# Graph attention and hyperbolic mean on one core: mask work and split parts moved to GpSimd, shorter scalar chains, and another opening of the mean

## The reference, cut to what matters

```python
h = jnp.maximum(_layernorm(x, axis=-1), 0.0)
x = x + _L0_gnn_ref(h, adj, adj, ptr, Wq, bq, Wk, bk, Wv, bv)
h = jnp.maximum(_layernorm(x, axis=-1), 0.0)
x = x + _L1_gnn_ref(h, adj, W)

# layer 0
a = jnp.where(mask, query @ key.T * scale, 0.0)
scores = (a + b + edge_encoding) * jnp.where(mask, 1.0, -1000000.0)
softmax = jax.nn.softmax(scores, axis=-1) * mask
return softmax @ value

# layer 1
XW = mobius_matvec(W, X)                    # scalars: sqrt, artanh, tanh of each point's norms
gamma = jnp.maximum(2.0 / (1.0 + KAPPA * jnp.sum(X * X, axis=-1, keepdims=True)), 1e-15)
denom = _clamp_abs(A @ (gamma - 1.0))
nom = A @ (gamma * X)
two_mean = nom / denom                      # then more scalars of each point
```

## Time and profile before

| | us |
|---|---|
| median of 3 runs | 844.17 |
| lowest and highest run | 841.47, 846.86 |
| profiled execution | 846.85 |
| its span, first to last instruction | 845.0 |

### The profile page before, as it was taken

One profiled execution on the slowest core, in us unless ns is written; L12 is line 12 of the kernel. 1 busy time (PEld: TensorE's weight loads), 2 busy tenths in 40 slices (PEclk: granted clock), 3 DMA queues, 4 the chain that ended last, 5 costly groups with the idle time before them and its releaser, 6 DMA issues.

```text
span 845.0 us, 14675 instructions
## 1 busy us (share of the span) xinstructions
PE 754.9 (89%) x4989; PEld 693.3 (82%) x4996; DVE 667.2 (79%) x1371; ACT 478.9 (57%) x866; POOL 66.0 (8%) x128
## 2 busy tenths in 40 slices
PE   4999889999999997988639699999999999999980
PEld 4888667788778886876538699999999999999980
DVE  6778567887887886878629978888988888888874
ACT  3444366677677676858334355555555555445853
POOL 0000010100010100130200200000000000000080
PEclk9999989999999998998959899999999999999995
DMA  5115276777667774754950859999999999998632
GB/s 137 51 53 223 109 293 220 265 289 285 234 238 252 266 281 161 254 195 102 226 125 1 177 115 208 197 198 202 193 196 193 191 193 190 194 211 177 146 127 75
DMA packets 53574, 157.24 MB, mean 186 GB/s; under 512 B 9232, under 2 KB 30992, under 8 KB 47376
## 3 DMA queue, kind: packets, MB, share of 16 engines
q1 hardware_dynamic: 53520, 156.60, 69.5%
HBM read 148.16 MB, written 8.42 MB: 185 GB/s over the span
## 4 chain that ended last, share of the span: by engine, by line
PE 59%; DVE 20%; DMA 6%; issue 6%; ACT 4%; DVEq 4%; SPq 1%; ACTq 0%
PE bank L630 49%; PE bank L762 5%; DVE least L1458 4%; DMA adjL<-in_adj 3%; DMA adjU<-in_adj 2%; DVE adjT_lo L1398 2%; DVE least L1442 2%; PE bank L696 2%; PE bank L748 1%; DVE X_lo L1378 1%; DVE bank L1390 1%; DVE v L1262 1%; DVE scores L1415 1%; ACT adjT_hi L951 1%; PE bank L622 1%
## 5 line engine op out<-in xcount | busy, mean ns | idle before, releaser
L630 PE MATMUL bank<-X_hi,adjT_hi 128*128 128x258 f32 x1024 | 292.0, 285 | 28.5 <-DVE adjT_lo L1398 28.3
L630 PE MATMUL bank<-X_lo,adjT_hi 128*128 128x258 f32 x1024 | 291.9, 285 | 0.0
L630 PE MATMUL bank<-X_hi,adjT_lo 128*128 128x258 f32 x1024 | 291.3, 284 | 0.0
L630 PEld LDWEIGHTS bank<-X_hi,adjT_hi 128*128 128x128 f32 x1024 | 195.5, 191 | 30.7 <-issue 23.6
L630 PEld LDWEIGHTS bank<-X_lo,adjT_hi 128*128 128x128 f32 x1024 | 196.0, 191 | 0.0
L630 PEld LDWEIGHTS bank<-X_hi,adjT_lo 128*128 128x128 f32 x1024 | 195.8, 191 | 0.0
L762 PE MATMUL bank<-values,probT 128*128 128x256 f32 x512 | 123.1, 385 | 4.4 <-ACT probT L991 4.4
L951 ACT CAST adjT_hi<-turned 128x1024 fp32r<-128x1024 f32 x64 | 67.1, 1048 | 75.9 <-PE bank L630 57.4
L762 PEld LDWEIGHTS bank<-values,probT 128*128 128x128 f32 x512 | 94.5, 193 | 18.2 <-ACT probT L991 5.5
L951 ACT CAST adjT_hi<-bank 128x1024 fp32r<-128x1024 f32 x64 | 64.8, 1013 | 69.3 <-PE bank L630 45.3
L1398 DVE TENSOR_TENSOR adjT_lo<-turned,adjT_hi 128x1024 fp32r<-128x1024 f32 x64 | 77.7, 1215 | 21.7 <-ACT adjT_hi L951 21.5
(11 more groups left out here) (172 smaller groups left out, 1117.6 us busy)
## 6 DMA issues: line engine op xcount, KB each, us to landing
adjL<-in_adj SPq DMA_DIRECT2D x120, 512.0 KB, 8.8
adjU<-in_adj SPq DMA_DIRECT2D x32, 1024.0 KB, 6.1
adjL<-in_adj SPq DMA_DIRECT2D x16, 2048.0 KB, 10.2
x_scratch<-x SPq DMA_DIRECT2D x16, 258.0 KB, 3.6
xin<-in_x SPq DMA_DIRECT2D x8, 512.0 KB, 3.8
xt<-in_x SPq DMA_DIRECT2D x16, 256.0 KB, 4.4
adj<-in_adj SPq DMA_DIRECT2D x8, 512.0 KB, 12.4
x_all<-x_scratch SPq DMA_DIRECT2D x16, 256.0 KB, 11.0
```

What stands on the lines that cost most here:

```text
L630: last = pe.matmul(dst, a[i][a_cols], b[j][b_cols], start=(k_first and n == 0), stop=(k_last and n == 2))
```

## The change

- GpSimd makes `same`, `factor`, `far_part` and the overwritten columns of each lower tile (`mask_lower`), one step ahead; VectorE waits for `s_same` and `s_pushed`.
- The points have two batches of 16 columns. The chain of a batch is written with fewer operations. That of the first batch is spread over steps 11 to 14: two parts between the second and third read of scores, four between `tiles_out` and `maximum_lower`. Its 16 pieces are scaled and split wholly by GpSimd (`points_whole`): six ahead of the own mask of step 14, ten behind it. The second chain runs after the attention, among the first chunks of the mean.
- The mean opens with four tiles: 16 chunks, the two early quarters of the tiles 0 to 3 first. GpSimd takes the low part of the chunks 3, 5, 7, 9 and 11 (`adj_low_beside`).
- In the last step ScalarE copies the first two turned groups ahead of the exponentials of the last lower tile. SyncE loads the first tile of the mean before the store of x1. ScalarE issues the last two stores of x1, and VectorE copies half of the last norms straight from `x1`.
- The mean's code is written twice, once in the If body and once under Else (`mean_part`), except SyncE's. The jump now stands at the end of the mean.

```diff
-    BATCH_END = (PAIRS // 2, PAIRS - 2, PAIRS)
+    BATCH_END = (PAIRS // 2, PAIRS)
...
-    FIRST_CHUNKS = ([(t, q) for t in range(3) for q in range(2)] + [(t, q) for q in range(2, NQ) for t in range(3)])
+    FIRST_CHUNKS = ([(t, q) for t in range(4) for q in range(2)] + [(t, q) for q in range(2, NQ) for t in range(2)]
+                    + [(t, q) for t in range(2, 4) for q in range(2, NQ)])
     FIRST = len(FIRST_CHUNKS)
+    POOL_LOW = tuple(range(3, FIRST - 4, 2))
...
+                    if is_step(s, HT - 1):
+                        sp.wait_ge(s_expL, HT - 1)
+                        mean_adj(0, first_adj[0], d_adj[0])
...
-                x1_store(step_at(HT - 2))
                 sp.wait_ge(s_expL, HT)
                 mean_adj(2, first_adj[2], d_adj[1])
-                x1_store(step_at(HT - 1))
-                norms_back(PAIRS - 1, HT)
+                sp.wait_ge(s_x1_last[0], 16)
+                for a in range(0, QD, 2):
+                    norms_of(PAIRS - 1, a, s_norms[1])
                 sp.wait_ge(s_qk, (HC + 1) * HT)
...
+            def points_whole(pieces):
+
+                pool.wait_ge(s_scale, 1)
+                for m, u in pieces:
+                    t = u * PAIRS + m
+                    always(pool)
+                    pool.tensor_scalar(product[:, t, 0:D], product[:, t, 0:D], 0.0, v[8][:, t:t + 1], ALU.add, ALU.mult)
+                    pool.drain()
+                    pool.tensor_copy(X_hi[:, t, 0:D], product[:, t, 0:D])
+                    pool.drain()
+                    pool.tensor_tensor(X_lo[:, t, 0:D], product[:, t, 0:D], X_hi[:, t, 0:D].bitcast(F32),
+                                       ALU.subtract).then_inc(s_early, 1)
...
+            def adj_low_beside(n):
+
+                slot = n % 4
+                pool.wait_ge(d_hi, n + 1)
+                always(pool)
+                pool.tensor_tensor(adjT_lo[slot][:, :, :].rearrange("p k c -> p (k c)"), turned[slot],
+                                   adjT_hi[slot][:, :, :].rearrange("p k c -> p (k c)").bitcast(F32), ALU.subtract)\
+                    .then_inc(d_lo_beside, 1)
...
+            def mean_part():
+
+                for n in POOL_LOW[:3]:
+                    adj_low_beside(n)
+                points_high(4)
+                points_high(5)
+                adj_low_beside(POOL_LOW[3])
+                points_high(6)
+                points_high(7)
+                for n in POOL_LOW[4:]:
+                    adj_low_beside(n)
+
...
+                def mask_lower(s):
+
+                    low = s.tile(HALFWAY)
+                    pool.wait_ge(s_adjL[s.par], turns(s))
+                    always(pool)
+                    pool.tensor_scalar(same[:, s.par, :], graph_t[:, low, :], graph_col[:, bass.ds(low, 1)], None,
+                                       ALU.is_equal).then_inc(s_same, 1)
+                    pool.drain()
+                    pool.tensor_scalar(factor[:, :], same[:, s.par, :], 1.0 - FAR, FAR, ALU.mult, ALU.add)
+                    pool.drain()
+                    wait(pool, s_maxL, s.n)
+                    always(pool)
+                    pool.tensor_tensor(far_part[:, :], adjL_t[:, s.par, low, :], factor[:, :], ALU.mult)
+                    pool.drain()
+                    pool.tensor_copy(adjL_t[:, s.par, low, :], pushed[:, :]).then_inc(s_pushed, 1)
+
...
+                    if is_step(s, HT - 2):
+                        points_whole(EARLY_PIECES[:BEFORE_LAST])
...
+                        pool.drain()
+                        mask_lower(s.plus(1))
                     if is_step(s, HT - 2):
-                        points_high(0)
...
-                pe.wait_ge(d_lo, n + 1)
+                    pe.wait_ge(s_early if q < 2 else s_lo, KB * (q % 2 + 1))
+                    pe.wait_ge(s_edge, q // 2 + 1)
+                if isinstance(n, int) and n in POOL_LOW:
+                    pe.wait_ge(d_lo_beside, POOL_LOW.index(n) + 1)
+                else:
+                    pe.wait_ge(d_lo, low_count(n))
...
+                first_chunk(1)
+                pe.wait_ge(s_mx, HT)
+                for n in range(2, FIRST):
...
                 steps(pe, step)
-                product(step_at(HT - 3), HT - 1)
                 pe.wait_ge(s_x1, T - 2)
                 first_chunk(0)
-                turn_cent(step_at(HT - 1), HT - 2)
+                turn_cent(step_at(HT - 1), HT - 3, 0)
...
+                        if c == 2 and last_step:
+                            exp_own(s)
+                            exp_lower(s)
+                        elif c == 2 and after(s, 2):
+                            product_out(s.plus(-3))
+                        if c == 3 and last_step:
                             cent_squares(s.plus(-1))
-                        if last_step and c == 4:
-                            point_function(1, BATCH_COLS[1])
-                        if c == 2 and after(s, 2):
-                            product_out(s.plus(-3))
+                            x1_store(s.plus(-1))
+                        if c == 4 and last_step:
+                            adj_high(0)
                         b = (s.par * (HC + 1) + c) % 2
                         width = CH if c < HC else P
...
+                        product_out(s.plus(-3))
                     if after(s, 0):
...
+                adj_high(1)
+                cent_squares(step_at(HT - 1))
+                x1_store(step_at(HT - 1))
+                cent_copy(step_at(HT - 1), 0)
+                adj_high(2)
                 product_out(step_at(HT - 3))
-                cent_squares(step_at(HT - 1))
-                cent_copy(step_at(HT - 1))
                 product_out(step_at(HT - 2), 6)
-                product_out(step_at(HT - 1), 7)
+                product_out(step_at(HT - 1), 0)
+                act.wait_ge(s_norms[1], 16 * (QD * (PAIRS - BATCH_END[0]) - QD // 2))
+                act.wait_ge(s_beside_norms, 1)
+                mean_part()
             with act.Else():
...
+                dve.drain()
+                tt(v5, v4, v4, ALU.mult)
+                dve.drain()
+                dve.scalar_tensor_tensor(out=v5, in0=v5, scalar=-0.5, in1=msq_slots[c], op0=ALU.mult, op1=ALU.mult)
+                dve.drain()
+                function_done()
+                tt(v6, v3, v3, ALU.mult)
+                tt(v0, v3, v4, ALU.mult)
+                dve.drain()
+                tt(v6, v6, v5, ALU.mult)
+                dve.drain()
+                ts(v6, v6, 0.5, None, ALU.add)
+                dve.drain()
+                dve.reciprocal(v6, v6)
+                dve.drain()
+                dve.scalar_tensor_tensor(out=v8, in0=v6, scalar=1e-15, in1=v0, op0=ALU.max, op1=ALU.mult).then_inc(s_scale, 1)
...
+                first_turn(3)
+                adj_low(2)
+                first_turn(4)
+                dve.drain()
+                first_turn(5)
+                points_norms(1)
+                points_series(1)
+                adj_low(4)
+                points_ratio(1)
+                points_argument(1)
+                first_turn(6)
+                points_factor(1)
+                adj_low(6)
+                points_edge(1)
+                first_turn(7)
+                points_low(4)
+                points_low(5)
+                first_turn(8)
+                adj_low(8)
+                first_turn(9)
+                points_low(6)
+                points_low(7)
+                for n in range(10, FIRST):
+                    first_turn(n)
+                    if n not in POOL_LOW:
+                        adj_low(n)
+                adj_turn(4, 0, 0, FIRST)
+                mean_scales(0, 2, 2)
...
                 def scores_lower(s):
 
-                    low = s.tile(HALFWAY)
-                    wait(dve, s_own_m, s.n - 1)
-                    dve.tensor_scalar(same[:, s.par, :], graph_t[:, low, :], graph_col[:, bass.ds(low, 1)], None, ALU.is_equal)
-                    dve.drain()
-                    dve.tensor_scalar(factor[:, :], same[:, s.par, :], 1.0 - FAR, FAR, ALU.mult, ALU.add)
+                    dve.drain()
+                    dve.wait_ge(s_same, s.n + 1)
                     dve.wait_ge(s_qk, (HC + 1) * s.n + HC + 1)
...
                 def maximum_lower(s):
 
-                    low = s.tile(HALFWAY)
                     dve.wait_ge(s_adjL[s.par], turns(s))
-                    dve.tensor_tensor(far_part[:, :], adjL_t[:, s.par, low, :], factor[:, :], ALU.mult)
-                    dve.drain()
-                    dve.tensor_copy(adjL_t[:, s.par, low, :], pushed[:, :])
+                    dve.wait_ge(s_pushed, s.n + 1)
...
+                def early_points(s, parts, first):
+
+                    for n, part in enumerate(parts):
+                        if is_step(s, first + n):
+                            part(0)
...
+                        scores_upper(s.plus(1), lambda: early_points(s, (points_norms, points_ratio), HT - 5))
...
```

(5 more changed lines are left out.)

647 lines of the change are left out of this document (314 added, 333 removed).

## The result

| | us |
|---|---|
| before, median of 4 runs | 842.99 |
| after, median of 4 runs (830.73 to 834.0) | 833.21 |
| ratio, 95% interval | 0.9863, 0.9827 to 0.9899 |
| profiled execution of after, and its span | 832.69, 830.8 |

The change makes the kernel 1.4% faster. The prediction was 815, with a range from 801 to 830, so the measured 833.21 lies outside it. The span fell from 845.0 to 830.8, by 14.2 where 30 was forecast. The changed kernel has another line numbering: the minima are lines 1706 and 1719, the low parts of `adj` 1528 on VectorE and 594 on GpSimd, its matmuls 708.

A forecast was written before the change was run, and what follows sets the result against it. Attention was bound by a ring of VectorE and TensorE, the mean by TensorE, with a tail between. 5.4 (masks) + 3.9 (first chain) + 21.6 (tail) - 1 = 30 us off 846.85 gave 817, at the median 815; range 801 to 830.

The forecast's parts named there:

- the ring: Attention step: VectorE's minima and mask, score read and TensorE's next product wait on each other; TensorE's 17.4 us and a transfer limit it.
- The price of a piece: GpSimd's list in the tail: each piece of points, three operations with drains, takes 1.85 us.
- the time of the own mask: Tail: GpSimd's mask of step 15 is ready 13.5 us behind the last lower minimum.
- the masks: Attention steps: moving lower tile masks off VectorE saves 0.45 us in each of 12 steps, 5.4 us, bounds 0 to 9.
- The steps don't get shorter: Rival for attention: the upper tile's transfer holds the period, so moving the masks gives 0; 820 us, chance 0.04.
- the first chain: Steps 11 to 14: spreading its scalar operations saves 3.9 us, bounds 0 to 8; 61 us for three steps.
- centring at 19.5: Tail: the last centring starts 19.5 us behind the last lower minimum instead of 35.0, with GpSimd's mask late next.
- the 6.20 for the first tile: Tail: VectorE's wait of 6.20 us for the mean's first tile goes, as that loads before the stores of x1.
- 19.1 us lost: Mean's opening behind the second chunk: TensorE loses 19.1 us, waiting for chunks 3, 7, 8, 9 and 10, against 12.7 before.
- The rival in which GpSimd bounds the tail: Tail: pieces of 2.4 us and low parts of 2.7 delay the mask and four chunks; 826 us, chance 0.15.
- Part D: Mean: the jump at its end and squares ahead of a cast in the 17th chunk cost 1 us, bounds 0 and 4.85.
- VectorE and GpSimd hold each other up: Rival: GpSimd's pieces and low parts slow VectorE's operations beside them through shared ports; 827 us, chance 0.12.

The follow-up runs named there:

- e7: The kernel before, with the rest of the next upper tile issued ahead of the store of x1 and the load of x: 842.56 us.
- e8: e2 with the mask work of the lower tiles back on VectorE: 834.24 us.
- e1: The changed kernel with the mask work of the lower tiles back on VectorE: 839.01 us.
- e2: The changed kernel with the rest of the next upper tile issued ahead of the store of x1 and the load of x: 821.29 us.
- e12: The changed kernel with a second buffer for the last x1, so VectorE needn't wait for the store of the last but one: 823.36 us.
- e4: The changed kernel with GpSimd making the high parts of late points ahead of its low part of chunk 7, of last points ahead of chunk 9's: 827.03 us.
- e10: e5 with ScalarE's squares of the means of tiles 0 and 1 moved from ahead of chunk 16's cast to the last four tiles: 807.69 us.
- e5: The changed kernel with upper tile ahead of x1 store, third tile's loads behind last but one x1 store, GpSimd's high parts first: 812.61 us.
- e9: The changed kernel with the low parts of chunks 3, 5, 7, 9 and 11 made by VectorE instead of GpSimd: 829.89 us.

## Why the prediction was wrong

**Right.** The steps were held by two limits, as the prediction said of the ring; e7 and e8 show both. The price of a piece (1.87 for 1.85) and the time of the own mask (12.4 for 13.5). A GpSimd low part takes 2.37 us (2.2 taken, 2.0 to 2.7 given). No wait behind a jump before the second chunk.

**Right in size, by luck: the masks.** 5.4 was forecast and e1 found 6.5 to 7.2, but the 5.4 was 0.45 in each of 12 steps, and a step got only 0.23 to 0.29 shorter. In the ordinary steps the transfer held nearly all of it back, as the rival "The steps don't get shorter" has it; what makes up for it is above all the first step. With the transfer out of the way (e8 to e2) the ring gives 0.63 a step. Of the first chain the three steps came out (60.7 for 61), but the fourth step that it touches, 2.4 us longer, stood in no sum.

**Wrong: the last centring, "centring at 19.5".** What is late next was not GpSimd's mask but the store of the last but one x1. I took the 6.20 for the first tile off the path, and of the loads that now stand ahead of the store I counted none against it. The code has the wait in plain sight: one x1 buffer, whose store must have landed. Term: 25.7 measured, 17.7 without it (e12), worth 9.1 us (7.6 by the ratios). Without that wait the path is the one forecast, mask and then centring, and even shorter.

**Wrong: "19.1 us lost" behind the second chunk.** 27.1 were, or 23 without the wait for chunk 16. Some 5 us of it (5.5, or 4.4 by the ratios) is the high parts behind a low part in GpSimd's list (e4). The rival in which GpSimd bounds the tail had GpSimd and the points queued in it, but named slow pieces and slow low parts as the reason, and they were as fast as forecast; their order was bad.

**Mis-sized: Part D.** Squares ahead of the cast of chunk 16 were put at 1 us with the jump. They cost 4.9 (e10 against e5; 4.3 by the ratios), the jump at the end nothing.

The three together are 9.1 + 5.5 + 4.9 = 19.5, or 16.3 by the ratios, and the forecast was missed by 833.2 - 815 = 18.2. So they are about as large as the miss. That they explain all of it is not shown: no run has just these three, and e12 takes away 8.0 us of centring where the forecast was off by 6.2.

**In part: VectorE and GpSimd hold each other up.** It happens, and bigger than the rows of before showed: `v<-v` of 16 columns at 416.62 lasts 2.37 us, just as long as GpSimd's low part at 416.59, and the five operations at 419.32 take 3.34 together, beside the low part at 420.25. In e9, without low parts on GpSimd, the same operations take:

```profile
419.83 0.18 DVE L1372 TENSOR_TENSOR v<-v 128x16 f32<-128x16 f32 x1
...
420.34 1.18 DVE L1432 SCALAR_TENSOR_TENSOR v<-v 128x16 f32<-128x16 f32 x5
```

That makes 4.4 us, in a chain for whose end the late points and the turn of chunk 7 wait. What it costs the kernel no run shows by itself: e9 takes it away, and the low parts ahead of the high parts with it, but gives VectorE five low parts; its 2.6 us are what is left of all three. The Trainium skill ("SBUF — State Buffer", "Who interferes with whom") says that a VectorE instruction with two inputs in SBUF contends with a GpSimd instruction that reads there, and that the ports that they share are locked exclusively; by that rule, the trace agrees, with 2.37 beside 2.37. The lower minimum at 377.96 ran beside GpSimd's pieces and took 4.42, as in the earlier trace rows; the same section of the Trainium skill says that `tensor_reduce` never contends on this chip.

**What stayed open.** The jump's cost in a kernel without the other waits; what the held up chain costs; and the part of e12's gain that the clock has (the products took 1.5 us less at the higher one, not measured by itself).
